# Turning a quad's maxima ahead of step 4's values, copying them ahead of the exponential, with a lead of 26 tiles

## What is computed

```python
x = x + 0.5 * _L0_ffn_ref(_layernorm(x), w_gate, w_up, w_down)
x = x + _L0_attn_ref(_layernorm(x), Wq, Wk, Wv, Wo, bo)
x = x + 0.5 * _L0_ffn_ref(_layernorm(x), w_gate, w_up, w_down)
# attention, H = 16 heads of D = 16:
scores = einsum('bhld,bhsd->bhls', qh, kh) * D ** -0.5 + bias   # bias = -slope * |i - j|
attn = softmax(scores, axis=-1)
out = einsum('bhls,bhsd->bhld', attn, vh) ... @ Wo.T + bo
# ffn, 256 -> 768 -> 256:
h = silu(x @ wg.T) * (x @ wu.T);  return h @ wd.T
```

## Time and profile before

| | us |
|---|---|
| three runs | 866.61, 871.42, 865.44 (median 866.61) |
| the profiled execution | 867.33 |
| its span, first to last instruction | 865.5 |
| mean granted clock of TensorE | 0.986 of full speed |
| attention, first to last exponential | 198.9 to 698.3, about 62.6 a sequence |

### The profile page before, as it was taken

The page is one execution under the profiler, slowest core; times in us unless marked ns, Lnnn a source line. Parts: engine busy times, 40 slices in busy tenths (PEclk is TensorE's granted clock), DMA queues, the critical chain, the costliest instruction groups (busy, mean ns, idle before and its releaser), DMA issues.

```text
span 865.5 us, 13038 instructions
## 1 busy us (share of the span) xinstructions
PE 782.1 (90%) x4576; PEld 487.6 (56%) x4576; DVE 650.7 (75%) x1347; ACT 514.5 (59%) x745; POOL 432.2 (50%) x486
## 2 busy tenths in 40 slices
PE   2699999998999999999998998999898898889997
PEld 2578887864443454453453444444453357778886
DVE  5488977768898778778778878778788357467764
ACT  4334444335667777778777777777577664334443
POOL 0343345343545655665665665665554454344433
PEclk9799999999999999999999999999899999999999
DMA  9330025303730721622522422424320000000001
GB/s 366 113 41 3 2 32 79 42 2 41 107 43 6 106 39 24 90 38 37 77 38 39 75 38 52 64 36 65 49 38 3 1 2 25 27 27 27 27 27 50
DMA packets 21491, 43.18 MB, mean 50 GB/s; under 512 B 3848, under 2 KB 5912, under 8 KB 21208
## 3 DMA queue, kind: packets, MB, share of 16 engines
q1 hardware_dynamic: 21400, 41.92, 26.4%
HBM read 12.02 MB, written 4.62 MB: 19 GB/s over the span
## 4 chain that ended last, share of the span: by engine, by line
PE 64%; DVE 13%; issue 10%; ACT 8%; DMA 2%; SPq 1%; POOL 1%; DVEq 0%; ACTq 0%
PE ps L955 59%; ACT probs L642 4%; DVE row_max L822 3%; DVE hid L756 3%; PE ps L1018 2%; DMA q_scale<-q_scale 2%; PE ps L967 1%; DVE newton L688 1%; ACT stage L602 1%; ACT stage L599 1%; DVE xnt L878 1%; DVE rstd L690 1%; DVE newton L686 1%; ACT max_row L617 1%; SPq L365 1%
## 5 line engine op out<-in xcount | busy, mean ns | idle before, releaser
L822 DVE TENSOR_REDUCE row_max<-ps 128x1 f32<-128x512 f32 x512 | 332.8, 685 | 92.1 <-PE ps L955 89.7
L642 ACT ACTIVATE probs<-ps 128x1024 f32<-128x1024 f32 x256 | 260.1, 1024 | 135.8 <-PE ps L955 135.1
L525 POOL TENSOR_TENSOR probs<-probs,diag 128x256 f32<-128x256 f32 x256 | 187.9, 735 | 200.4 <-ACT probs L642 200.4
L457 POOL TENSOR_TENSOR hid_r<-hid,hid_r 128x512 fp32r<-128x512 f32 x96 | 124.8, 1302 | 194.5 <-ACT hid_r L551 193.7
L955 PE MATMUL ps<-xnt,wgu_r 128*128 128x512 f32 x768 | 194.2, 406 | 19.4 <-DVE hid L756 14.2
L955 PE MATMUL ps<-k_aug,q_aug 60*128 60x512 f32 x512 | 205.2, 467 | 6.7 <-DVE row_max L822 6.7
L955 PE MATMUL ps<-q_aug,k_aug 62*128 62x512 f32 x512 | 201.1, 458 | 7.2 <-ACT probs L642 7.1
L955 PEld LDWEIGHTS ps<-xnt,wgu_r 128*128 128x128 f32 x768 | 144.2, 192 | 60.7 <-DVE hid L756 19.5
L955 PEld LDWEIGHTS ps<-q_aug,k_aug 62*128 62x128 f32 x512 | 81.3, 185 | 150.7 <-issue 128.8
L955 PE MATMUL ps<-probs,v_aug 128*32 128x512 f32 x1024 | 137.2, 608 | 1.1 <-POOL probs L525 0.9
L557 ACT ACTIVATE gated<-ps 128x512 f32<-128x512 f32 x96 | 57.4, 599 | 132.2 <-PE ps L955 123.1
(11 more groups left out here) (72 smaller groups left out, 669.1 us busy)
## 6 DMA issues: line engine op xcount, KB each, us to landing
q_aug<-parts SPq DMA_DIRECT2D x96, 128.0 KB, 4.2
k_aug<-parts SPq DMA_DIRECT2D x96, 128.0 KB, 4.7
x_sb<-x_in SPq DMA_DIRECT2D x8, 512.0 KB, 12.9
x_out<-x_sb SPq DMA_DIRECT2D x8, 512.0 KB, 2.7
diag<-diag_table SPq DMA_DIRECT2D x1, 2048.0 KB, 18.8
wgu_i<-w_gate_up SPq DMA_DIRECT2D x2, 768.0 KB, 6.0
w_att<-w_att SPq DMA_DIRECT2D x1, 1024.0 KB, 11.3
q_aug<-max_row SPq DMA_DIRECT2D x64, 8.0 KB
```

The source lines that it names most:

```text
L457: nc.gpsimd.tensor_tensor(hid_r[:, 1, f, :], hid[:, f % 2, :], hid_r[:, 0, f, :].bitcast(F32), ALU.subtract).then_inc(s["hid_lo"], 1)
L525: nc.gpsimd.tensor_tensor(tile, tile, diag[:, kt % 2, n * QH + 2 * pair:n * QH + 2 * pair + 2, :], ALU.mult).then_inc(fixed, 1)
L642: nc.scalar.activation(probs[:, kt % 2, 2 * pair:2 * pair + 2, :], ps[:, at:at + 2, :], ACT.Exp, scale=SLOPE_UNITS[pair]).then_inc(exp_don ...
L822: nc.vector.reduce_max(row_max[:, quad % 2, i, pair, t:t + 1], max_bank(tile), mybir.AxisListType.X).then_inc(s1_used, 1)
```

## The change

The fill "max" of step 4 is put ahead of the values instead of behind the step's second maxima tile, and ScalarE copies it ahead of step 4's exponential instead of behind it. All other fills are emptied where they were, behind their own step's exponential; `drain` is only cut in two, `empty` and `round_hi`. The maxima run 26 tiles ahead rather than 24, so that a quad's last tile comes in step 2, not 3; two more tiles are made in the last but one sequence of stage A. VectorE makes the rest of an "xt" two steps behind the fill, not three. In steps that have no maxima tile (the last 13 of the attention, before this change 12) the second half of the scores now comes right behind the first.

```diff
--- before.py
+++ after.py
@@ -130,14 +130,14 @@
 FIRST_AT = {(4, 4): "qk0_next", (4, 5): "qk1_next", (5, 0): "v0_next", (5, 1): "v1_next", (5, 2): "qk2_next", (5, 3): "qk3_next"}
 
 FIRST_MAX_AT = {(B - 3, 5): range(0, 2), (B - 2, 0): range(2, 4), (B - 2, 2): range(4, 6), (B - 2, 4): range(6, 8),
-                **{(B - 1, f): range(2 * f + 8, 2 * f + 10) for f in range(FT)}}
-FIRST_MAX_DOWN = {2: range(20, 22), 4: range(22, 24)}
+                (B - 2, 5): range(8, 10), **{(B - 1, f): range(2 * f + 10, 2 * f + 12) for f in range(FT)}}
+FIRST_MAX_DOWN = {2: range(22, 24), 4: range(24, 26)}
 FIRST_V = 5
 LAST_BLOCKS_AT = {(2, 3): 0, (2, 6): 1, (3, 1): 2, (3, 3): 3}
 APPLY_AT = {(1, 2): 0, (1, 4): 1, (1, 6): 2, (2, 2): 3}
 FIRST_ROWS_C_AT = {(1, 3): 0, (1, 6): 1, (2, 3): 2, (3, 1): 3}
 PLACE_AT = {(3, 4): 0, (3, 5): 1, (3, 6): 2}
-DIVIDE_LATER, SPLIT_LATER = 2, 3
+DIVIDE_LATER, SPLIT_LATER = 2, 2
 FIRST_FILLS = [f for f in ALL_FILLS if not f.endswith("_prev")]
 
 LAST_FILLS = [f for f in ALL_FILLS if not f.endswith("_next") or f.startswith("xt")]
@@ -153,7 +153,7 @@
 
 
 MAX_TILES = 2 * NQ * STEPS
-MAX_LEAD = 24
+MAX_LEAD = 26
 
 
 def max_tiles_at(b, step):
@@ -586,7 +586,8 @@
             act.wait_ge(dn_in, 16)
             nc.scalar.copy(wdn_r[:], wdn_i[:]).then_inc(w_ready, 1)
             turned(0, 0)
-            def drain(b, name):
+            def empty(b, name):
+
                 at = fill_no(b, name)
                 seq, kind, part = fill_parts(b, name)
                 bank = bank_of(b, name)
@@ -600,12 +601,6 @@
                                              ).then_inc(drained, 1)
                     else:
                         nc.scalar.copy(stage[:, slot_of(b, name), :], bank).then_inc(drained, 1)
-                    if kind in SPLIT:
-
-                        if kind == "qk":
-                            wait(act, rows_moved[part % 2], (seq * CHUNKS + part // 2) * MOVES)
-                        act.wait_ge(drained, at + 1)
-                        nc.scalar.copy(hi_and_lo(name)[0], stage[:, slot_of(b, name), :]).then_inc(split_hi, 1)
                 elif kind == "v":
                     if not (isinstance(seq, int) and seq == 0):
                         act.wait_ge(v_ready, NQ * seq)
@@ -616,6 +611,20 @@
                     wait(act, max_moved, quad_no * (16 * 2))
                     nc.scalar.copy(max_row[:, :], bank[0:2 * TT * QH, 0:P]).then_inc(drained, 1)
 
+            def round_hi(b, name):
+
+                seq, kind, part = fill_parts(b, name)
+                if kind in SPLIT:
+                    if kind == "qk":
+                        wait(act, rows_moved[part % 2], (seq * CHUNKS + part // 2) * MOVES)
+                    act.wait_ge(drained, fill_no(b, name) + 1)
+                    nc.scalar.copy(hi_and_lo(name)[0], stage[:, slot_of(b, name), :]).then_inc(split_hi, 1)
+
+            def drain(b, name):
+
+                empty(b, name)
+                round_hi(b, name)
+
             act.wait_ge(watt_in, 16)
             nc.scalar.copy(wqkv[:, 0, :, :], w_att[:, :, 0:3 * C]).then_inc(watt_hi, 1)
             nc.scalar.copy(wo[:, 0, :, :], w_att[:, :, 3 * C:4 * C]).then_inc(watt_hi, 1)
@@ -635,6 +644,11 @@
                         kt, pair = s // 2, s % 2
                         quad_no = b * NQ + n
                         g = quad_no * STEPS + s
+                        name = FILLS.get((n, s))
+                        name = name if name in fills_of(b) else None
+                        fill_first = name and name.startswith("max")
+                        if fill_first:
+                            empty(b, name)
                         act.wait_ge(st_done, g + 1)
 
                         wait(act, pv_done, quad_no * TT + kt - 1)
@@ -643,9 +657,10 @@
                                              ACT.Exp, scale=SLOPE_UNITS[pair]).then_inc(exp_done, 1)
                         if s == 2 and not (first(b) and n == 0):
                             take_heads(quad_no - 1)
-                        name = FILLS.get((n, s))
-                        if name in fills_of(b):
-                            drain(b, name)
+                        if name and not fill_first:
+                            empty(b, name)
+                        if name:
+                            round_hi(b, name)
 
             turns(act, turn)
             take_heads(B * NQ - 1)
@@ -1168,8 +1183,12 @@
                         tiles = max_tiles_at(b, n * STEPS + s)
                         name = FILLS.get((n, s))
                         scores(b, n, s, 0)
+                        if not tiles:
+                            scores(b, n, s, 1).then_inc(st_done, 1)
                         scores_for_max(b, tiles[:1])
                         if s % 2 == 0:
+                            if name in fills_of(b):
+                                fill(b, name)
                             if s >= 4:
                                 weigh_values(quad_no, n, (s - 4) // 2, b)
                             elif not (first(b) and n == 0):
@@ -1178,10 +1197,9 @@
                             if first(b) and (n, s) == (0, 1):
                                 pe.wait_ge(ffn[0]["y_used"], 2 * B)
                             fill(b, name)
-                        scores(b, n, s, 1).then_inc(st_done, 1)
+                        if tiles:
+                            scores(b, n, s, 1).then_inc(st_done, 1)
                         scores_for_max(b, tiles[1:])
-                        if s % 2 == 0 and name in fills_of(b):
-                            fill(b, name)
 
             for b in range(B):
                 turn(b)
```

## The result

| | before | changed |
|---|---|---|
| median of the runs | 866.03 us (861.86 to 871.42, 4 runs) | 887.15 us (882.55 to 892.11, 4 runs) |
| ratio | | 1.024, 95% interval 1.016 to 1.032 |
| profiled execution's span | 865.5 us | 885.7 us |
| mean granted clock of TensorE | 0.986 | 0.981 |
| first exponential of the fourth sequence to that of the fifth | 62.57 us | 65.47 us |

What follows compares the result with a forecast made beforehand. TensorE, busy 90%, with step 5's "heads" waiting for ScalarE's `max_row` copy. 12.2 + 3.5 + 3.0 + 0.2 + 1.6 - 0.45 - 3.6 = +16.5 us gave 883.1 us, 1.9% slower; range 873 to 890.

Steps and rivals of the forecast that it cites:

- The stall: Step 4: "max", ahead of the values, stands 1.43 us for the copy of step 3's fill; E4 at E3 + 3.33.
- One sign had been named as "wrong": Wrong if E3 to E4 under 2.5 us in quads 2 and 3, "max" stall under 1 us, or E5 to E6 still 1.65.
- What is late next: Behind "heads", VectorE's maxima tiles: E4 to E5 1.25 us, E5 to E6 2.05 to 2.09 instead of 1.65.
- the rival "only the stall": VectorE's tiles don't bind behind "heads"; only the stall costs, +6 to +7 us, 873 us; chance 0.15.
- Quads 0 and 1: Steady sequences: step 3's copy already has a rounding behind it, so +0.5 us a quad, 7 x 0.5 = +3.5 for quads 1.
- The "xt" rest: Made a step sooner beside GpSimd's multiplication; quad 0's wait moves from `xnt` to `row_max`, +0.5 us each, +3.0 for six.
- The lower of the two prices, by free overlap: "xt" rest: if VectorE and GpSimd didn't hinder each other, quad 0 would cost about +0.1 us instead of +0.5.
- The term of +1.6 for quad 0: First sequence, quad 0: 1.15 us lost nearly whole behind "max" (E6 +1.1), and 0.6 more for the "xt" rest.
- Last sequence: Quad 1 gains 0.45 us; from quad 2, step 3, twelve intervals take 16.8 instead of 20.2 us, in all -3.6 there.
- The term of quad 1: Last sequence, quad 1: no fill at step 3, so E3 to E6 falls by some 0.45 us (bounds 0 and 0.95).
- small thing: Small things: negation a step sooner 0, two tiles moved into stage A 0 (at most +1.4 us), the maxima's DMAs 0.
- The rival that "heads" would be freed at no price: No stall at "max": each steady quad gains 0.45 to 0.5 us, some 16 us in all, 850 us; chance 0.06.

Runs made afterwards that it cites:

- E4: Not a run: the start of the exponential of step 4 in a quad.
- E3: Not a run: the start of the exponential of step 3 in a quad.
- E6: Not a run: the start of the exponential of step 6 in a quad.
- The kernel before with one more tile: The kernel before with step 5's first tile reduced twice, 32 more reductions of 0.685 us on VectorE: 866.67 us in one run.
- both traces of the changed kernel: The changed kernel's profiled execution (span 885.7 us) and a second trace of it, unedited: 883.69 us.
- The experiment with step 3's copy: The changed kernel with ScalarE also emptying step 3's fill ahead of step 3's exponential; 851 us expected, 862.87 us measured, ratio 0.997 to the kernel before.
- the one with "max" behind the values: The changed kernel with the turned maxima behind step 4's values, ahead of the second scores; 857 us expected, 862.57 us measured, ratio 0.997 to the kernel before.
- E5: Not a run: the start of the exponential of step 5 in a quad.
- E2: Not a run: the start of the exponential of step 2 in a quad.
- the short multiplication: The changed kernel with GpSimd's multiplication of step 4 of quad 0 cut from 128 to 16 columns a head: 877.70 us in one run.
- the kernel with the copy alone and pairs: The kernel before with ScalarE's max_row copy ahead of step 4's exponential, and second scores right behind the first in steps without maxima tiles: 840.98 us, ratio 0.970.
- the changed one with one more tile: The changed kernel with step 5's first tile reduced twice, 32 more reductions of 0.685 us on VectorE: 909.51 us in one run.

## Why the prediction was right

**The sum, stretch by stretch.** The two profiled executions lie 20.2 us apart, where the sum had 16.5:

| stretch | in the sum | measured |
|---|---|---|
| up to the first exponential | 0 | +1.3 us |
| first sequence | +3.0 | +6.9 |
| second to sixth | +14.4 | +15.7 |
| seventh | +2.9 | -1.9 |
| last sequence and stage C | -3.9 | -1.8 |

The mechanism of a steady quad was right. That the total came out within 4 us is in part luck: the terms for the first, the seventh and the last sequence missed by 3.9, 4.8 and 2.1 us, and the seventh missed the other way.

The seventh sequence is not a steady one, though the text before the prediction says that all but the first and the last are alike. In the kernel before it took 68.91 us, not 62.6. In its quad 2 VectorE's normalisation stood ahead of a tile, and the negations behind it took 0.64 and 0.65 us beside GpSimd's work; the turned maxima came only at E4 + 2.65 us (TensorE had idled 1.24 us), and then the clock was at 1.2 GHz for 6.8 us, from 616.7; E3 to E6 took 10.47 us instead of 5.66. The granted clock of that sequence was 0.95:

```profile
575.00:643.90 68.90, 63.39 (x366) 30.25 (x364) 55.62 (x106) 47.20 (x65) 38.11 (x49) 0.95 0.33 47
```

The kernel before with one more tile shows the same (10.45 us there). In both traces of the changed kernel the clock is 1.00 throughout that sequence and the quad takes 7.13 us. How much of this is the order's doing and how much the clock's, no run separates.

**The stall.** "max" at E3 + 1.57 and E4 at E3 + 3.33 were predicted; 1.55 and 3.30 were measured, in quads 1 to 3 of the sequence shown. The experiment with step 3's copy shows the cause, and the one with "max" behind the values what it costs. One sign had been named as "wrong": a stall of "max" under 1 us. By the rows it was met in quads 0 to 2, where "max" waited 0.98, 0.87 and 0.48 us; only quad 3 has 1.78. There TensorE had already waited 0.54, 0.74 and 1.12 us with the tile ahead of "max", which the prediction didn't have. The time is the same, since bank 7 was the last of the two to come free.

**What is late next.** 1.25 and 2.05 to 2.09 were predicted, 1.24 and 2.09 measured; E6 at E3 + 6.63 in both. The step rested on a likeness, steps 0 and 1 of quad 0, and held because all that sets the pace there (four transposes, then values, four tiles on VectorE) was the same. The added reductions show for quads 1 to 3 that it is VectorE. The rival "only the stall" falls.

**Quads 0 and 1.** +0.5 each was predicted. With E3 to E6 at 6.65 and 6.62 us against 6.06 and 6.10, and the start of the step 7 fill, a steady sequence came to +2.90; predicted were 0.5 + 0.5 + 0.94 + 0.94 = 2.88.

**The "xt" rest.** The wait for `xnt` did turn into one for `row_max`, and the fill of step 7 came at E5 + 2.79, where 2.85 was predicted. The lower of the two prices, by free overlap, is refuted. The Trainium skill's rule (SBUF — State Buffer, "SBUF: two separate sides") gave the right one, and the overlaps of 1.13 us and 0.68 us shown above agree with it as well.

**First sequence.** The term of +1.6 for quad 0 was too small for these traces by 3.8 us: E2 to E3 took 1.98 us and E3 to E6 9.37 at the lower clock, against 0.93 and 6.64 with the short multiplication, where that stretch had the full clock. There the stall part holds: 6.64 is 1.06 above the 5.58 before, where 1.1 had been forecast.

**Last sequence.** Predicted were 16.8 us for the twelve intervals; 17.0 were measured in the kernel with the copy alone and pairs, 17.6 in the changed one. The term of quad 1 failed. A gain of 0.45 us from E3 to E6 was predicted there; it took 7.99 us, where it was 5.77 before. E3 to E4 alone took 3.98 us, where it was 1.79 before, and 3.88 in the second trace. The clock was at 1.2 GHz from 688.6 for 3.4 us, but that is the smaller part: in the kernel with step 3's copy ahead, which has the same order in this quad and had the full clock there, E3 to E4 took 3.59 us and E3 to E6 6.93. In this quad and in quad 2 no fill at step 3 hides the negation. VectorE in quad 1, with E3 at 685.64:

```profile
684.89 0.84 DVE L847 TENSOR_SCALAR max_in<-row_max 128x16 fp32r<-128x16 f32 x1
685.77 0.65 DVE L849 SCALAR_TENSOR_TENSOR max_in<-row_max,max_in 128x16 f32<-128x16 f32 x1
686.34 1.96 DVE L837 TENSOR_REDUCE row_max<-ps 128x1 f32<-128x512 f32 x3
```

GpSimd:

```profile
684.43 1.27 POOL L481 TENSOR_TENSOR att_t<-stage,att_t 128x512 fp32r<-128x512 f32 x1 [0.40 <-ACT att_t L621]
685.66 0.72 POOL L525 TENSOR_TENSOR probs<-probs,diag 128x256 f32<-128x256 f32 x1
```

and TensorE:

```profile
687.07 0.18 PEld L970 LDWEIGHTS ps<-k_aug,q_aug 60*128 60x128 f32 x1 [1.56 <-DVE row_max L837]
687.50 0.10 PEld L1028 LDWEIGHTS ps<-eye,max_in 128*32 128x32 f32 x1 [0.25 <-issue]
```

Step 4's first tile waits 1.56 us for its bank, since step 3's is only reduced behind the late negation, and "max", the values and the scores stand behind it. With a lead of 24 (and "max" behind the values) the same interval is 2.04 us. So the step that failed is a "small thing": "Negation comes a step sooner, where VectorE waits for tiles: 0". It was right where the stall of "max" hid it. From E3 to E4 it cost some 1.8 us here at full clock, and 0.6 us in quad 2, where "max" itself came late. It also is most of why my forecasts for the kernels without the stall, 851 and 857 us, came out 12 and 6 us too low; the first one had the lower clock for 13.7 us in its last sequence besides, and 0.47 us in each quad 0.

The rival that "heads" would be freed at no price needed bank 7 empty 1.4 us sooner. Its chance of 0.06 was fair for the change as made, but the gain it spoke of was there for the half of the change that leaves TensorE's order alone.

## What to carry to other kernels

When a fill is moved ahead of other work on an engine in order, ask what its wait is hidden by now: here the values covered 1 us of a wait for a shared PSUM bank, and moved ahead of them the fill stalled them as well. To free a consumer, first move the producer's copy alone, and leave the order of the busiest engine as it is; that gained 2.4% here, and the whole change lost 2.4%. And a wait that is removed may have hidden others: look at which engine was catching up in that time.

## What the runs showed of the hardware

- Some operations of VectorE on SBUF waited for GpSimd's, even tiny ones: negations of 16 elements a partition took 1.07 and 0.65 us instead of 0.17, and ended 0.03 to 0.04 us behind GpSimd's 1.30 and 0.73 us operations, which had begun first. The first of them reads a single tensor. A rest of 512 elements ended 0.55 us behind GpSimd's, whether it had begun 0.13 us (1.13 us long) or 0.56 us behind GpSimd's start (0.71 us long).
- TensorE's clock fell to its lower level, 1.2 GHz, in every trace, inside the run for 3.4 to 13.7 us at a time; mean granted clocks lay between 0.969 and 0.990. The kernel with most idle time on TensorE (97.6 us), the changed one with one more tile, had the lowest, and the fastest (57.7 us) the highest, but those between them don't follow this order: 85.2 us of idle time came with 0.986, and 70.9 with 0.979.
- Some falls stood at one place of the program. In the changed kernel the longest, 13.6 us, was in the first sequence's quad 0 in both traces. In the seventh sequence's quad 2 the kernel before and the same with one more tile both had 6.8 us; the changed kernel had none in either trace.
